# Layer norm of y where y is made for every second dense step, and first rows kept by masked sums in place of a dump of the running sums

## The reference

```python
def _mean_aggr(x, src, dst, n):
    s = segment_sum(x[src], dst, n)
    cnt = segment_sum(ones, dst, n)
    return s / max(cnt, 1)[:, None]

def _sage(x, src, dst, Wl, b, Wr):
    return _mean_aggr(x, src, dst) @ Wl.T + b + x @ Wr.T

h = relu(_sage(x, src, dst, W1l, b1, W1r))
out = _sage(h, src, dst, W2l, b2, W2r)
x = layernorm(x + out)
```

## Time and profile before

| | us |
|---|---|
| median of 3 runs | 3004.59 |
| the profiled execution | 3004.84 |
| its span, first to last instruction | 3003.0 |

### The profile page before, as it was taken

One profiled execution on the slowest core, in us unless ns is written; L12 is line 12 of the kernel. 1 busy time (PEld: TensorE's weight loads), 2 busy tenths in 40 slices (PEclk: granted clock), 3 DMA queues, 4 the chain that ended last, 5 costly groups with the idle time before them and its releaser, 6 DMA issues. The chain is left out here.

```text
span 3003.0 us, 51944 instructions
## 1 busy us (share of the span) xinstructions
PE 1805.3 (60%) x9371; PEld 1338.1 (45%) x9371; DVE 2230.8 (74%) x8474; ACT 2022.7 (67%) x5239; POOL 1891.8 (63%) x1802
## 2 busy tenths in 40 slices
PE   5666666444455443677777667666665666635552
PEld 4565655233333332445555433335554555524442
DVE  7978888766666663787878566666886888888883
ACT  5888878444344432788888688883554888858885
POOL 7777776588888886333333465537775766426775
PEclk8877777677767776798999888887998888755555
DMA  6989988333333333899999799996886888834441
GB/s 210 304 287 298 301 292 278 96 63 62 59 62 62 62 62 71 278 348 340 348 337 350 268 332 329 324 310 199 257 259 196 295 293 287 271 122 160 159 159 50
DMA packets 293472, 663.86 MB, mean 221 GB/s; under 512 B 55177, under 2 KB 88596, under 8 KB 293404
## 3 DMA queue, kind: packets, MB, share of 16 engines
q1 hardware_dynamic: 214587, 549.74, 52.8%
q0 software_dynamic: 78816, 113.45, 17.3%
HBM read 342.83 MB, written 324.08 MB: 222 GB/s over the span
## 5 line engine op out<-in xcount | busy, mean ns | idle before, releaser
L1211 ACT ACTIVATE node_out<-node_in,n_shift,n_root 128x128 f32<-128x128 f32 (+1 forms) x1176 | 468.2, 482 | 75.5 <-DVE n_shift L1516 74.6
L760 POOL DMA_INDIRECT sums<-gat_sums,dst_safe_i x196 | 185.1, 945 | 292.1 <-DVE pre L1862 237.8
L827 POOL DMA_INDIRECT gat_sums<-sums,add_idx x196 | 322.4, 1645 | 66.6 <-issue 58.5
L1499 DVE BATCH_NORM_STATS2 n_stats<-node_in 128x6 f32<-128x256 f32 (+1 forms) x784 | 279.2, 418 | 82.0 <-DMA node_in<-y_nodes 69.1
L880 POOL DMA_INDIRECT out_dram<-node_x2t,out_index x196 | 211.1, 1077 | 167.9 <-ACT node_x2t L1211 107.6
L768 POOL DMA_INDIRECT src_rows<-x_table,row_i x200 | 197.5, 988 | 134.3 <-issue 53.2
L768 POOL DMA_INDIRECT sums<-x_table,row_i x192 | 193.7, 1009 | 99.5 <-issue 50.0
L760 POOL DMA_INDIRECT own_rows<-x_table,row_i x196 | 191.1, 975 | 65.8 <-issue 54.2
L768 POOL DMA_INDIRECT own_rows<-in_x_dram,dst_safe_i x196 | 192.6, 983 | 59.7 <-issue 56.4
L760 POOL DMA_INDIRECT src_rows<-in_x_dram,src_i x196 | 191.1, 975 | 60.2 <-issue 58.7
L1220 ACT ACTIVATE t_a<-ps 128x512 f32<-128x512 f32 (+1 forms) x198 | 116.1, 587 | 149.3 <-PE ps L924 149.1
(11 more groups left out here) (359 smaller groups left out, 6548.7 us busy)
## 6 DMA issues: line engine op xcount, KB each, us to landing
x_table<-node_out SPq DMA_DIRECT2D x144, 512.0 KB
own_rows<-x_table SPq DMA_DIRECT2D x245, 256.0 KB, 3.0
node_in<-x_table SPq DMA_DIRECT2D x96, 512.0 KB
acc_dump<-acc SPq DMA_DIRECT2D x147, 264.0 KB
x_table<-new_rows SPq DMA_DIRECT2D x147, 256.0 KB
gat_sums<-node_x2t SPq DMA_DIRECT2D x49, 528.0 KB
node_sums<-gat_sums SPq DMA_DIRECT2D x48, 528.0 KB
node_in<-in_x_dram SPq DMA_DIRECT2D x48, 512.0 KB
```

The source lines that it names most:

```text
L760: g_.indirect_dma_start(out=to[:, g.b, j, 0:width], out_offset=None, in_=tab, in_offset=bass.IndirectOffsetOnAxis(ap=indices(j), axis=0)). ...
L827: g_.indirect_dma_start(out=gat_sums[:, :], out_offset=bass.IndirectOffsetOnAxis(ap=add_idx[:, g.b, j:j + 1], axis=0), in_=sums[:, g.b, j, ...
L1211: last = sc.activation(to[0:pn, g.b, j, :], rows[0:pn, g.b, j, 0:F], ACT.Identity, bias=NORM[k][2][0:pn, g.b, j:j + 1], scale=root[0:pn, j ...
L1499: last = v.bn_stats(NORM[k][0][0:pn, g.b, j:j + 2, :].rearrange("p j c -> p (j c)"), rows[0:pn, g.b, j:j + 2, 0:F].rearrange("p j f -> p f ...
```

## The change

1. In stage one, for even dense steps, y is no longer stored. DVE takes the moments of `node_y` (`even_moments`), ACT the root (`even_root`), DVE the shift (`even_shifts`), ACT writes the normalized rows into the buffer `gate` (`even_x3`), and SP stores them as x3 (`store_even_x3`).
2. In stage two the dense steps are the odd ones alone, 24 in place of 49, one each second iteration.
3. In stage two the running sums are not dumped. After each mean, DVE adds the running sum times the mask `first_done` to `fix_acc`, which then holds what the gather fetched; that gather and DVE's waits for the dumps are gone.

```diff
@@ def pipeline
+        for lag, stage, count, *half in stages:
+            t = s - lag
+            if half and t >= 0 and t % 2 == 0 and t // 2 < count:
+                stage(step(t // 2))
+            elif not half and 0 <= t < count:
+                stage(step(t))
...
+def even_only(stage):
+    def make(g):
+        if g.b == 0:
+            stage(g, Even(g.k, 0))
+    return make
@@ SP, stage one
             def store_y(g):
+                if g.b == 0:
+                    return
...
+            def store_even_x3(g, e):
+                wait_done(sp, flow["even3"]["m_row"], e)
+                for lo, hi in parts(g):
+                    sp.dma_start(node_rows(x3_table, SLOTS, g)[lo:hi], x3_even[lo:hi]).then_inc(even3_out, 16)
...
-            pipeline(sp, DENSE_FULL, [nodes(5, store_h1), nodes(5, store_y), nodes(3, store_nodes(D, x2_table, SLOTS))]
+            pipeline(sp, DENSE_FULL, [nodes(6, even_only(store_even_x3)), nodes(5, store_h1), nodes(5, store_y), nodes(3, store_nodes(D, x2_table, SLOTS))]
@@ SP, stage two
             pipeline(sp, DENSE_FULL, edges((0, load_own(L, L["tr_b"], x2_table, own_rows, L["own"])))
-                     + [nodes(0, load_nodes(D, y_nodes, 0, "n_row"))] + edges((1, dump))
-                     + [nodes(2, store_nodes(D, x3_table, SLOTS))] + edges((3, store)))
+                     + [odd_nodes(0, load_odd_y)] + [odd_nodes(2, store_odd_x3)] + edges((3, store)), per=4)
@@ POOL, the fix
-                wait_all(pool, L["dumped"])
-                g_.indirect_dma_start(out=fix_acc[:, :], out_offset=None, in_=acc_dump[:, :],
-                                      in_offset=bass.IndirectOffsetOnAxis(ap=fix_read, axis=0)).then_inc(fix_in, 16)
-                pool.wait_ge(fix_in, 16 * (n + 1))
+                if L is not flow["sage1"]:
+                    wait_all(pool, L["dumped"])
+                    g_.indirect_dma_start(out=fix_acc[:, :], out_offset=None, in_=acc_dump[:, :],
+                                          in_offset=bass.IndirectOffsetOnAxis(ap=fix_read, axis=0)).then_inc(fix_in, 16)
+                    pool.wait_ge(fix_in, FIX_IN_AT[n])
@@ ACT, stage one
+            def even_root(g, e):
+                wait_done(act, M["m_ve"], e)
+                at = NORM["m"][1][0:dense_p(g), 0, :]
+                sc.activation(at, at, ACT.Sqrt).then_inc(M["m_rt"].sem, 1)
+            def even_x3(g, e):
+                ...
+                wait_done(act, M["m_nm"], e)
+                for j in range(DJ):
+                    last = sc.activation(x3_even[0:pn, j, :], node_y[0:pn, 0, j, :], ACT.Identity,
+                                         bias=NORM["m"][2][0:pn, 0, j:j + 1], scale=NORM["m"][1][0:pn, 0, j:j + 1])
+                last.then_inc(M["m_row"].sem, 1)
             pipeline(act, DENSE_FULL, [
-                nodes(3, nodes_copy_x2t), nodes(4, nodes_copy_h1), nodes(3, nodes_relu),
+                nodes(3, nodes_copy_x2t), nodes(5, even_only(even_root)), nodes(4, nodes_copy_h1), nodes(3, nodes_relu),
                 nodes(2, normed_rows(D, "n", node_in, node_out, "n_row", "n_out", ("x2tp", "y")))]
                 + edges((2, normed_rows(L, "e", pre, new_rows, "newd", "stored")))
-                + [nodes(1, roots(D, "n"))] + edges((1, roots(L, "e"))))
+                + [nodes(5, even_only(even_x3)), nodes(1, roots(D, "n"))] + edges((1, roots(L, "e"))))
@@ DVE, stage one
-            pipeline(dve, DENSE_FULL, [nodes(2, shifts(D, "n"))] + edges((2, shifts(L, "e"))) + [nodes(4, nodes_y)]
-                     + edges((1, make_x2)))
+            pipeline(dve, DENSE_FULL, [nodes(2, shifts(D, "n"))] + edges((2, shifts(L, "e"))) + [nodes(5, even_only(even_shifts))]
+                     + [nodes(4, nodes_y), nodes(4, even_only(even_moments))] + edges((1, make_x2)))
@@ DVE, stage two
+            v.memset(fix_acc[:, 0:F], 0.0).then_inc(ones_set, 1)
+            v.tensor_scalar(fix_acc[:, F:F + 1], fix_skip[:, :], 1.0 / FAR, None, ALU.mult).then_inc(ones_set, 1)
+            def mean_and_first(j):
+                def make(g):
+                    ...
+                    made = v.tensor_scalar(msg[:, g.b, j, 0:F], acc[:, g.b, j, 0:F], edge4[:, g.b, 5, j:j + 1], None, ALU.mult)
+                    ...
+                    wait_part(dve, L["ended"], g, j)
+                    v.scalar_tensor_tensor(fix_acc[:, 0:F + 1], acc[:, g.b, j, 0:F + 1], one_of(first_done, g, j), fix_acc[:, 0:F + 1],
+                                           ALU.mult, ALU.add).then_inc(L["ended"].sem, 1)
-            pipeline(dve, DENSE_FULL, edges((0, plain_sums)) + [nodes(1, shifts(D, "n"))] + edges((0, means))
-                     + [nodes(0, node_moments(D))], per=4)
+            firsts = [(0, mean_and_first(j)) for j in range(J)]
+            pipeline(dve, DENSE_FULL, edges((0, plain_sums)) + [odd_nodes(1, shifts(D, "n"))] + edges((0, inverse_counts), *firsts)
+                     + [odd_nodes(0, node_moments(D))], per=4)
+            dve.wait_ge(L["ended"].sem, L["ended"].at(STEPS))
```

More of the change, by code:

```diff
@@ L183, in pipeline @@
 def pipeline(eng, looped, stages, per=2):
-    longest = max(lag for lag, _, _ in stages)
+    longest = max(lag for lag, *_ in stages)
     def at(s):
-        for lag, stage, count in stages:
-            if 0 <= s - lag < count:
-                stage(step(s - lag))
+        for lag, stage, count, *half in stages:
[4 more added lines that the diff above has]
+                stage(step(t))
     first = (longest + 3) // 2 * 2 if per == 2 else (longest + 5) // 4 * 4
@@ L202, in pipeline @@
                 t = first + h - lag
-                stage(Step(i * (per // 2) + t // 2, t % 2, t % 4, i + t // 4))
-    for s in range(first + per * loops, max(lag + count for lag, _, count in stages)):
+                if not half:
+                    stage(Step(i * (per // 2) + t // 2, t % 2, t % 4, i + t // 4))
+                elif t % 2 == 0:
+                    stage(Step(i + t // 4, t // 2 % 2))
+    for s in range(first + per * loops, max(lag + count * (2 if half else 1) for lag, _, count, *half in stages)):
         at(s)
@@ L224, in wide_edges, with index, odd_nodes @@
     return [(lag, stage, WIDE_STEPS) for lag, stage in stages]
+class Odd(Step):
+    def index(self):
+        return (2 * self.k + self.b) * 2 + 1
+class Even(Step):
+    def index(self):
+        return self.k
+def odd_nodes(lag, stage):
+    return (lag, stage, ODD_STEPS, True)
+def even_only(stage):
[3 more added lines that the diff above has]
+    return make
 def once(lag, stage):
@@ L445, in gnn_program @@
                            rings=dict(n_in=2, n_out=1, n_h1=1, n_y=1), steps=DENSE_STEPS),
-            "sage1": dict(back=["accd", "rcp", "msgd", "tr_a", "cp_a", "tr_b", "cp_b", "mm", "cp_c", "mm2", "newd"],
-                          rings=dict(own=1, dumped=1, stored=1), quads=dict(quad=J)),
-            "nodes3": dict(front=norm("n") + ["n_row"], rings=dict(n_in=1, n_out=1), steps=DENSE_STEPS),
+            "sage1": dict(back=["accd", "rcp", "msgd", "ended", "tr_a", "cp_a", "tr_b", "cp_b", "mm", "cp_c", "mm2", "newd"],
+                          rings=dict(own=1, stored=1), quads=dict(quad=J)),
+            "even3": dict(front=norm("m") + ["m_row"], rings={}, steps=EVEN_STEPS),
+            "nodes3": dict(front=norm("n") + ["n_row"], rings=dict(n_in=1, n_out=1), steps=ODD_STEPS),
             "sage2": dict(back=["accd", "rcp", "msgd", "tr_a", "cp_a", "tr_b", "cp_b", "mm", "pre", "newd", "e_cn"] + norm("e"),
@@ L472, in gnn_program @@
                     sems[n], counts[n] = sem2(n), [0, 0]
-                flow[layer][n] = Ring(sems[n], counts[n], m, steps, n in ("n_in", "n_out", "n_h1", "n_y"))
+                flow[layer][n] = Ring(sems[n], counts[n], m, steps, n in ("n_in", "n_out", "n_h1", "n_y") and steps == DENSE_STEPS)
                 counts[n] = flow[layer][n].end
@@ L1355, in _ @@
             D = flow["nodes3"]
-            pipeline(act, DENSE_FULL, [nodes(1, roots(D, "n"))] + edges((2, h1_rows))
-                     + [nodes(1, normed_rows(D, "n", node_in, node_out, "n_row", "n_out"))]
-                     + edges((1, sage_relu), (0, sage_copies)))
+            pipeline(act, DENSE_FULL, [odd_nodes(1, roots(D, "n"))] + edges((2, h1_rows))
+                     + [odd_nodes(1, normed_rows(D, "n", node_in, node_out, "n_row", "n_out"))]
+                     + edges((1, sage_relu), (0, sage_copies)), per=4)
             sage_copies(FIX, 1)
@@ L1886, in nodes_y @@
                 wait_done(dve, D["yp"], g)
-                wait_drained(dve, D["n_y"], g)
+                if g.b:
+                    wait_drained(dve, D["n_y"], g)
+                else:
+                    wait_previous(dve, flow["even3"]["m_row"], Even(g.k, 0))
                 for h in range(2):
```

54 lines of the change are left out of this document (47 added, 7 removed).

## The result

The changed kernel takes 3038.58 us (median of 5 runs, 3033.50 to 3040.50). The kernel before, run beside it, took 3005.47 (median of 5 runs, 3003.99 to 3019.88). The ratio on record is 1.0097, with a 95% interval of 1.0077 to 1.0116; it is not the quotient of the two medians, which is 1.0110; two of the five runs before took 3016.85 and 3019.88. Forecast were 3032 us and +0.9%.

The account below looks back on a forecast made before the run. Both touched stages looked bound by transfers, with ACT 0.6 us from being the bound in stage one. Stage one +72.7 and stage two -45.7 gave +27.0 us, 3032 us, slower by 0.9%; range 3000 to 3068.

Parts of the forecast that it names:

- Long iteration: Stage one, every second iteration: ACT's 9.25 us of ordered work plus 3.08 for eight normalizations, 12.33 us.
- Rival A: Stage one: ACT's 79 idle us absorb the added normalizations, so the kernel gets faster, 2969 us; chance 0.12.
- Short iteration: Stage one, the other iteration: DVE's moments and a possibly slow PE clock set it, 10.6 us, bounds 10.0 to 12.0.
- rival B: Stage one: PE's clock falls before each copy of a short iteration, +105 us there, total 3064; chance 0.15.
- point of decision, 11.3: Stage one: from a short iteration of 11.3 us on, rival B was to count as true.
- The lower end, 10.0: Stage one, short iteration: DVE's 8.3 us plus 1.7 for moments of y, 10.0, above ACT's 9.25.
- SP's queue: Stage one: the x3 store may hold back later stores and loads up to 4.6 us; cost put at nothing.
- Stage two, 5.5 a step: First SAGE aggregation: transfers stop binding, DVE becomes the bound; step from 6.41 to 5.5 us, 42.7 us less.
- masked chain: Stage two, DVE: four chained masked sums alternating with means, taken as 0.50 us apart, 2.1 us in all.
- C: Rival, about even: masked sums cost 0.39 us and stage two meets POOL's 5.0, total 3008 us; chance 0.14.
- D: Rival: masked chain costs 0.72 us or the removed transfers gave nothing, total 3074 us; chance 0.04.
- POOL's 5.0: Stage two: POOL's gathers at 1.255 us each need 5.0 us a step, a limit close behind DVE.

Follow-up runs that it names:

- E1: Changed kernel with the eight h1 transposes issued four times in even iterations, ahead of PE's gap; 3021.66 us, ratio 1.0037 to the kernel before.
- E4: Changed kernel with the first aggregation's running sums dumped and gathered again, no masked sums; 3036.93 us, ratio 1.0090 to the kernel before.
- E7: Changed kernel with the dump again, three even-step normalizations on ACT, five on DVE, even root last on ACT; 2970.20 us, ratio 0.9852.
- E8: E7's kernel with the eight h1 transposes issued twice in every even iteration; 2968.91 us, ratio 0.9858 to the kernel before.
- E9: Kernel before the change with the eight h1 transposes issued twice in every dense-stage iteration; 3018.85 us, ratio 1.0026.

## Why the prediction was right

The sign and the total held, and so did what bounds each stage, but for the short iterations. Two terms were mis-sized in opposite directions, by 22.7 and 16.4 us by stage, and 32.1 came out where 27.0 was forecast. With the first error alone the sum would have been +49.7, with the second alone +10.6: the sign does not hang on luck, the 5 us between forecast and measurement do.

- **Long iteration, 12.33.** 12.20. ACT sets it: its own order and the 3.08 us. Rival A, that idle time absorbs them, is refuted: ACT was busy 81% of the stage after, so idle time was left, and the stage still grew by 95 us.
- **Short iteration, 10.6 with bounds 10.0 to 12.0.** This is the first mis-sized term: 11.72, worth 1.12 x 23 = 25.8 us. The forecast held that the clock, at 0.92, would seldom be low at the copy. But with 3.80 us of waiting, where 2.9 was the longest before, it fell to 0.82 over the stage. By the prediction's own point of decision, 11.3, stage one is rival B's, and E1 shows the mechanism, with 10.39 once PE is kept at work; B's total of 3064 was missed because not every turn was slow and stage two saved more. The path was wrong as well, and with it the upper bound: the forecast counted only L1044 at the slow level, at 2.77 us for ACT. ACT's wait for it grew by 1.8 at most (2.91 in place of 1.10), and where it stayed at 2.58 or less and the transposes were in time it cost nothing, as DVE holds the iteration at 10.5 anyhow. Single short iterations took up to 13.15, since the second product and the transposes ran slow too, and ACT waited up to 2.15 us for its copy's input. ACT's total wait for L1101 was 79.2 us. By the rule of the Trainium skill that the prediction weighed (TensorE: Matmul & The Clock Gate, section HAM oscillation — how this bites in real kernels), a loop that leaves PE idle long enough on each turn starts each turn at the slow clock. The trace agrees in most turns and not in all: in 20 of the 23 short iterations L1101 was slow in whole or in part, in three it ran at full speed (1.98 or 1.99 us for the four) after the same wait of 3.80.
- **The lower end, 10.0.** DVE's 8.3 + 1.7 came out as 10.5 where nothing else held the iteration: ACT's roots wait for DVE's variances, and the copy stands behind the roots (1350.22 to 1350.50). The roots are 0.3 of the missing 0.5.
- **SP's queue, nothing.** No wait of DVE for the sums load appears in the stage; its waits for the x1 load add up to 2.0 us.
- **Stage two, 5.5 a step.** 5.15. The second mis-sized term, worth 16.4 us. The masked chain was priced rightly (0.50; 0.46 to 0.52 measured), and DVE is the bound: without the masked sums the stage is 8.6 us shorter (E4). POOL's 5.1 lies close behind. What came out shorter are the parts around it: four masked sums with their means 1910.34 - 1908.40 = 1.94 (forecast 2.1), sums to means 2.12 (2.24), statistics and variance 1.75 (1.87): 5.8 for a step with statistics (6.2). A step without them takes 4.26 (4.85): sums to means with the shifts 2.32 (2.54), and the same 1.94 (2.1 and 0.2 more). The two make 5.03 a step; some 0.1 is added by a pause of 0.40 in every fourth step and a few waits. The terms had been read where DVE waited for others between its instructions; that this is why they were long is argued, not shown.
- **C and D.** The masked sums did not cost 0.39, yet stage two came near POOL's 5.0: half of C. D is refuted by the step of 5.15 us.

What was not foreseen is that the two halves of the change are no sum. Either relieves the full DMA; the second one to come finds it relieved.

Left open: why three of the turns with a wait of 3.80 us kept the full clock for L1101; which part of the 0.6 to 1.1 us by which E7's pair exceeds its forecast is clock and which is DVE (89% busy, and 25.7 us of waits for x1 loads). E8 shows only that a short filler does not get it back. E7 changed the place of the rows, of the even root and the dump at once, so its gain is not divided among them. Why a fuller PE in E9 had a lower clock is open too.

## What to carry to other kernels

Before work is moved out of a transfer-bound stage, count how much room the engine that receives it has in the loop's order, waits included: 79 idle us held no room for 71, but a wait in the order, 1.1 us each turn, took three of the eight rows almost free (E7). A third engine that idles meanwhile may come back slower, and its slowness can spread to all it feeds for the rest of the iteration; price that for the whole chain, and not for the first product alone, whose slowness cost nothing by itself in five of the 23 short iterations. Where two savings relieve the same resource, time each alone and both: here the masked sums gained 0.6% alone and nothing beside the other.

## What the runs showed of the hardware

- After a wait of 3.80 us PE worked at the 1.2 GHz level for as long as 12 us, broken by one wait of 1.36 (1388.03 to 1399.82, granted clock 0.50), in other iterations for part of L1101 alone (3.41 us for the four), and in three of 23 not on L1101 at all (1.98 or 1.99). 24 more transposes ahead of the gap, which left the longest wait at 2.2 us, brought L1101's median from 697 to 592 ns.
- A fuller PE does not mean a higher clock: in E9 it had a fifth more instructions and was busy 87% of the stage, in place of 75% (slow work is itself a part of that), and the granted clock was 0.83 in place of 0.92.
- Eight rows of 128x128 with two column operands take 3.17 us on ACT and 2.14 on DVE.
- An independent 128x128 mean between two chained 129-column sums on DVE is free: the masked sums stay 0.46 to 0.52 us apart, where chained sums without it were 0.50 apart.
